# A four-layer graph network on one core: layers 0, 2 and 3 add their edges up as running sums on VectorE instead of scattering them on TensorE

## What is computed

```python
edge_index = jnp.stack([src, dst])
h = relu(layernorm(x)); x = x + L0(h, edge_attr_32, src, dst, ...)
h = relu(layernorm(x)); x = x + L1(h, ..., src, dst, edge_type_86)
h = relu(layernorm(x)); x = x + L2(h, edge_index, edge_weight, ...)
h = relu(layernorm(x)); x = x + L3(h, src, dst, ...)
# L0: msg = relu(h[src] + edge_attr);  agg = segment_sum(msg, dst);  ((1 + eps) h + agg) @ W.T + b
# L1: attention over 86 relations, 16 bases; the self loop takes the source of a node's LAST edge
# L2: msg = weight[:, None] * h[src];  agg = segment_sum(msg, dst);  relu(agg @ W + b)
# L3: msg = h[src];                    agg = segment_sum(msg, dst);  agg @ W.T + b
```

## Time and profile before

| | |
|---|---|
| median of the runs | 10135.78 us |
| the profiled execution, its own time / its span | 10080.74 us / 10078.9 us |
| busy share: PE / DVE / ACT / POOL | 43% / 44% / 22% / 66% |
| layer 0, first to last gather | 56 to 2404 us |
| layer 1 | 2404 to 5381 us |
| layer 2, first to last gather | 5381 to 7698 us |
| layer 3, first to last gather | 7740 to 10036 us |
| DMA share in the wide layers / in layer 1 | 0.09 to 0.16 / 0.74 |

### The profile page before, as it was taken

One profiled execution on the slowest core, in us unless ns is written; L12 is line 12 of the kernel. 1 busy time (PEld: TensorE's weight loads), 2 busy tenths in 40 slices (PEclk: granted clock), 3 DMA queues, 4 the chain that ended last, 5 costly groups with the idle time before them and its releaser, 6 DMA issues. The chain is left out here.

```text
span 10078.9 us, 104067 instructions
## 1 busy us (share of the span) xinstructions
PE 4355.2 (43%) x23835; PEld 3907.5 (39%) x23836; DVE 4409.0 (44%) x8833; ACT 2225.0 (22%) x5812; POOL 6679.0 (66%) x6577
## 2 busy tenths in 40 slices
PE   3444444445466666666663222222223232222333
PEld 2343443344366666666662222222222222222222
DVE  5444444444377777777774222222223122222222
ACT  1000000000377777777771000000000000000000
POOL 6666666664477777787775666666665666666665
PEclk6555555555655555555555555555555555555556
DMA  4111111111477777777772000000000000000001
GB/s 72 22 22 22 22 22 22 22 22 25 157 218 218 220 219 219 218 221 219 217 219 51 11 11 11 11 11 12 11 11 16 11 11 11 11 11 11 11 11 16
DMA packets 599592, 726.36 MB, mean 72 GB/s; under 512 B 339548, under 2 KB 433308, under 8 KB 596385
## 3 DMA queue, kind: packets, MB, share of 16 engines
q0 software_dynamic: 290064, 544.60, 22.0%
q1 hardware_dynamic: 309497, 181.39, 6.6%
HBM read 685.53 MB, written 40.64 MB: 72 GB/s over the span
## 5 line engine op out<-in xcount | busy, mean ns | idle before, releaser
L511 POOL DMA_INDIRECT lanes<-table,idx x4764 | 4510.3, 947 | 2539.4 <-issue 1430.4
L1277 PE MATMUL ps<-arena 128*128 128x128 f32 x9528 | 2376.9, 386 | 4187.7 <-issue 4124.4
L1277 PEld LDWEIGHTS ps<-arena 128*128 128x128 f32 x9528 | 2037.9, 277 | 4483.2 <-issue 4397.9
L511 POOL DMA_INDIRECT arena<-table,idx x1664 | 2050.8, 1232 | 675.8 <-issue 508.9
L987 DVE TENSOR_TENSOR ps<-ps,tabs 128x16 f32<-128x16 f32 x1191 | 210.5, 177 | 4057.4 <-remote 3303.4
L586 ACT COPY idx<-tabs 128x4 int32 (+1 forms) x1191 | 228.2, 193 | 6715.6 <-DMA lanes<-table,idx 6484.7
L992 DVE TENSOR_TENSOR arena<-ps,node 128x512 f32<-128x512 f32 (+1 forms) x1588 | 1056.8, 682 | 83.0 <-issue 82.2
L1269 PE MATMUL ps<-lanes 128*128 128x32 f32 x3328 | 791.6, 402 | 664.1 <-issue 463.5
L1269 PEld LDWEIGHTS ps<-lanes 128*128 128x128 f32 x3328 | 750.2, 330 | 691.5 <-issue 691.3
L1377 PE MATMUL ps<-t,arena 128*128 x3328 | 955.0, 402 | 0.0
L1377 PEld LDWEIGHTS ps<-t,arena 128*128 128x128 f32 x3328 | 860.0, 318 | 0.0
(11 more groups left out here) (201 smaller groups left out, 2807.1 us busy)
## 6 DMA issues: line engine op xcount, KB each, us to landing
arena<-step_rows SPq DMA_DIRECT2D x416, 256.0 KB
lanes<-table,idx POOLq DMA_INDIRECT x4764
arena<-table,idx POOLq DMA_INDIRECT x1664
table<-arena SPq DMA_DIRECT2D x24, 1088.0 KB, 5.2
lanes<-in_edge_attr SPq DMA_DIRECT2D x384, 64.0 KB
table<-h SPq DMA_DIRECT2D x18, 256.0 KB, 2.4
edge_rows<-arena SPq DMA_DIRECT2D x1, 2496.0 KB, 8.4
lanes<-self_loop_table,selfi POOLq DMA_INDIRECT x98
```

Of the source, the lines that this page charges most:

```text
L511: pool.indirect_dma_start(out=into, out_offset=None, in_=tableD[l], in_offset=bass.IndirectOffsetOnAxis(ap=index, axis=0)).then_inc(there, 16)
L1277: last = mm(ps[:, bass.ds(w[u], WB * D)], onehotw[:, k, u, :], wmsg[:, k, u].rearrange("p w f -> p (w f)"), start=False, stop=True, skip_g ...
```

## The change

The edges are dealt out anew in the wide layers. Partition p holds the run of consecutive edges p x 1563 to p x 1563 + 1562, so tile t is the t-th edge of all 128 partitions, and there are no extra tiles. Because edges are sorted by destination, each partition's edges come in runs of one node. Per tile DVE updates a row that holds four entries (`KEEP`): the running sum of the present node and the final sums of the three nodes before. With `same` = 1 if the edge's node is that of the edge before, the new row is `prev * same + terms`, where the terms are the edge's own message and the older entries moved along, times `1 - same`. In layer 0 an entry also carries the node's number and the source of its last edge (34 wide instead of 32).

ACT writes the messages into PSUM (`fill`), double buffered by lots, and the two factors into `scal`. SP stores every lot of rows to HBM (`put_sums`, 1563 x 128 rows of 544 or 512 bytes a layer). When the layer is through, 25 indirect gathers (`gather_fours`) fetch, for every four nodes, the row after the last edge that can belong to them; DVE picks the four sums out of the row (`pick`), PE adds what the next partition continues (`place_ends`) and moves the sums to blocks (`to_blocks`, 16 small matmuls a bank), and `linear` goes on as before. Which rows to fetch is found during layer 0: a comparison in 25 of its rounds and 25 extra gathers in the middle (`look_up`).

The core of it (the one-hots, masks, `scatter`, `clear`, the wide window tables and the extra tiles are gone):

```diff
-WB = 4
-WIDE_LOTS = -(-(TILES + EXW) // HB)
+KEEP = 4
+QB = -(-BLOCKS // 4)
+WIDE_LOTS = -(-TILES // HB)
+WIDTH = {0: D + 2, 2: D, 3: D}
 # VectorE
-            def masks(l, i, k):
-                dve.wait_ge(wide_mm_done, lots_to(l, i, k))
-                tt(mask[:, k], ..., ALU.is_equal).then_inc(masked, 1)
-            def body3(i, lots_):
-                for k in range(lots_):
-                    masks(3, i, k)
-                    onehots(i, k, onehotw)
-                    rows_there(3, i, k)
-                    dve.wait_ge(masked, lots_to(3, i, k))
-                    spread(k, grow, mask)
+            def chain(l, i, k):
+                w = WIDTH[l]
+                dve.wait_ge(filled, i * RING + (BEFORE[l] + k + 1 + RING))
+                if l:
+                    dve.wait_ge(ring_moved[k], written_count(l, i, k))
+                for u in range(tiles_of(i, k)):
+                    prev = ringA[l][:, k, u - 1] if u else ringA[l][:, (k - 1) % RING, HB - 1]
+                    terms = new(l, k)[:, u // 2, u % 2]
+                    dve.wait_ge(link, link_count(l, i, k, u))
+                    ts(terms[:, w:KEEP * w], prev[:, 0:(KEEP - 1) * w], scal[:, k, 1, u:u + 1], None, ALU.mult
+                       ).then_inc(link, 1)
+                    dve.wait_ge(link, link_count(l, i, k, u) + 1)
+                    stt(ringA[l][:, k, u], prev, scal[:, k, 0, u:u + 1], terms, ALU.mult, ALU.add).then_inc(link, 1)
 # ScalarE
+            def fill(l, i, k, ahead):
+                act.wait_ge(wide_gathered[k], gathered_count(l, i, k))
+                if ahead:
+                    wide_lot(i, k + RING)
+                act.wait_ge(link, link_count(l, i, k - 1, 0))
+                m = same[:, bass.ds(i * ROUND + k * HB, HB)]
+                nc.scalar.copy(scal[:, k, 0, :], m)
+                nc.scalar.activation(scal[:, k, 1, :], m, ACT.Relu, scale=-1.0, bias=ones[:, 0:1])
+                ...
+                    nc.scalar.copy(to[:, :, :, 0:D], grow[:, k].rearrange(...)).then_inc(filled, 1)
 # SyncE
+            def put_sums(l, i, k):
+                w, nt = KEEP * WIDTH[l], tiles_of(i, k)
+                sp.wait_ge(link, link_count(l, i, k, nt))
+                sp.dma_start(sumsD[l]...[:, bass.ds(i * ROUND + k * HB, nt), :], ringA[l][:, k, 0:nt]
+                             ).then_inc(ring_moved[k], 16)
 # GpSimd
-                        pool.wait_ge(total_ready if l == 0 else wide_msg_ready, n)
+                        pool.wait_ge(total_ready if l == 0 else filled, n)
+            def gather_fours(l):
+                for k in range(RING):
+                    pool.wait_ge(ring_moved[k], 16 * (1 + (TURN[l] + 2) * (ROUNDS + (1 if k < REST else 0))))
+                for b in range(BANKS):
+                    for B in fours_of(b):
+                        pool.indirect_dma_start(out=fours[l][:, B, :], ..., in_=sumsD[l], in_offset=...rowE[:, B:B + 1]...)
 # TensorE
-            def scatter(l, i, k, w):
-                pe.wait_ge(wide_msg_ready, i * RING + (BEFORE[l] + k + 1 + RING))
-                for u in range(HB):
-                    last = mm(ps[:, bass.ds(w[u], WB * D)], onehotw[:, k, u, :], wmsg[:, k, u]..., start=False, ...)
+            def to_blocks(l, b):
+                pe.wait_ge(quads_ready, PICKS[l] + b + 1)
+                clear(b)
+                ... for q in range(4): for i in range(4):
+                            last = mm(to, spread_of(q, i), quads[:, i, B[0]:B[-1] + 1], start=False, ...)
```

More of the change, by code:

```diff
@@ L118, in gnn @@
         tT = sb("tT", [P, GROUPS * P])
[L120 to L130, removed]
+        tabs = sb("tabs", [P, 2, STEPS_N])
+        idxS = sb("src_rows", [P, T4], I32)
+        same = sb("same", [P, T4], BF16)
+        wgt = sb("wgt", [P, T4])
+        has_edge = sb("has_edge", [P, QB * 4])
+        selfi = sb("selfi", [P, QB * 4], I32)
+        RSRC, DST, ETY = range(3)
         window = sb("window", [1, STEPS_N], I32)
@@ L537, in _ @@
                         narrow(n)
+                    continue
+                if l == 0:
+                    with pool.Fori(0, FOUND_ROUND) as i:
+                        wide(i, RING)
+                    look_up()
+                    with pool.Fori(FOUND_ROUND, ROUNDS) as i:
+                        wide(i, RING)
                 else:
@@ new lines, in wide_layer, with add @@
+            def wide_layer(l):
+                zero_sums(l)
+                with dve.Fori(0, ROUNDS) as i:
+                    for k in range(RING):
+                        chain(l, i, k)
+                for k in range(REST):
+                    chain(l, ROUNDS, k)
+            def add(i, k):
+                dve.wait_ge(wide_gathered[k % RING], gathered_count(0, i, k))
+                dve.wait_ge(ring_moved[k % RING], written_count(0, i, k))
+                dve.wait_ge(filled, i * RING + (k + 1 + LOTS))
+                tt(total[:, k % LOTS], grow[:, k % RING], attr[:, k % RING], ALU.add).then_inc(total_ready, 1)
@@ new lines, in compare, with rounds0 @@
+            def compare(i, k):
+                if k == 0:
+                    ts(compared, ends, thr4[:, bass.ds(i, 1)], None, ALU.is_lt).then_inc(compare_done, 1)
+                if k == RING // 2:
+                    dve.wait_ge(compare_done, i + 1)
+                    nc.vector.reduce_sum(tile4[:, bass.ds(i, 1)], compared, AX.X).then_inc(compare_done, 1)
+            def rounds0(i, n, also=None):
+                for k in range(n):
+                    if also:
+                        also(i, k)
+                    if not isinstance(i, int) or i * RING + k + 1 < WIDE_LOTS:
+                        add(i, k + 1)
+                    chain(0, i, k)
@@ L1297, in transposes, with sources_to_blocks @@
+            def sources_to_blocks():
+                pe.wait_ge(quads_ready, BANKS + 1)
+                clear(7)
+                for q in range(4):
+                    for i in range(4):
+                        last = mm(ps[:, SRC7:SRC7 + 4 * QB].rearrange("p (B q) -> p B q", q=4)[:, :, q], spread_of(q, i),
+                                  fours_src[:, i], start=False, stop=True, skip_group_check=True)
+                last.then_inc(permuted, 1)
             def transposes(of, b):
@@ L1303, in _, with linear @@
             tf, hf = (v[:, :, :].rearrange("p b f -> p (b f)") for v in (t, h))
-            def linear(q, w, bias):
+            def linear(q, w, bias, l=None):
+                if l is not None:
+                    place_ends(l)
+                    to_blocks(l, 0)
+                    to_blocks(l, 1)
                 for turn in range(BANKS + 1):
+                    if l is not None and turn + 2 < BANKS:
+                        to_blocks(l, turn + 2)
+                    if l == 0 and turn + 2 == BANKS - 1:
+                        sources_to_blocks()
                     if turn < BANKS:
```

795 lines of the change are left out of this document (443 added, 352 removed).

## The result

The changed kernel takes 10393.6 us (median of 4 runs, 10392.5 to 10412.6), the kernel before 10136.6 us beside it (4 runs, 10115.1 to 10140.4): ratio 1.0262, 95% interval 1.0244 to 1.0281, slower. The forecast was 10331 us. The profiled execution has a span of 10391.9 us for 10078.9, +313 us, so the 55 us between the old profile and its median have no counterpart here.

The account below looks back on a forecast made before the run. POOL's gather stream, 1.25 us apart with holes, was taken to bound the kernel. Gathers -26, ends +180, `look_up` +31 and preparation +10 gave +195 on 10081, 10276; plus 55 for the median, 10331 us, range 10110 to 10750.

Parts of the forecast that it names:

- The chain: DVE's two dependent instructions a tile, 285 and 266 ns: 2.4 to 2.8 us a lot, hidden behind POOL's 5.0.
- The slow lot: DVE's cost of four tiles while instructions issue late in the wide layers: 8.5 to 10 us, against 2.4 to 2.8 otherwise.
- The gaps of 0.5 us: Sign in DVE's instruction stream: gaps by "issue" when instructions come late, against 0.03 us in fast phases.
- The pace: Wide-layer gathers stay at 1.479 us each including holes: 4689 gathers take 6935 us, -26 us; bounds 1.25 and 1.75.
- The ends: Between a layer's last gather and the next layer's first: 100 us for 42.5, +58 a layer, +180 with layer 0's sources.
- the drain of the backlog with the last store: At a wide layer's end, DVE finishes up to 8 lots and the last store lands: 12 + 2 us.
- PE as the end's bound: At a layer's end PE's moving of sums, 8.4 us a bank, outlasts DVE's picks, 6.2: 50 us for six banks.
- Preparation: Work before layer 0's first tile, whose parts change: +10 us, between -10 and +30.
- The 55 us added for the median: Whole kernel: the median of the runs lies 55 us above the profiled execution, so 10276 became 10331 us.
- Rival A: Wide layers: with PE silent the slow phases go, 1.25 us a gather, 9186 us in all; chance 0.28.
- Rival B: Wide layers: DVE's issue falls to about 1 us an instruction, a lot takes 7 us, 11580 us in all; chance 0.13.
- Rival C: Whole kernel even: 1.446 us a gather and ends at +135 give 10111 us, the forecast's lower edge; no separate chance.

Follow-up runs that it names:

- the pauses: Changed kernel with a POOL memset of 256, 512 or 1024 columns after each lot's wide gathers: 10284.7, 10529.9 and 11035.8 us for 10071.3 of the kernel before.
- second profile: The changed kernel run again unedited, beside the kernel before on the same chip: 10341.1 us for 10084.5, ratio 1.0254.
- the second set: Runs with lighter POOL pauses in both kernels, or the changed kernel with fewer rows, instructions or stores; unpaused kernel before 8911.0 us, paused 8995.0.

## Why the prediction was right, and where it was off

The direction, the range and the main reading were right: POOL's stream stays, its stops stay, and the ends pay. The forecast of 10331 us was 63 us low, which is the sum of misses of both signs.

- Gathers, 1563 a layer at 947 ns and 1.25 us apart: right.
- The chain. 0.61 us a tile was forecast, 0.74 measured (323 and 350 ns for 266 and 285), 3.0 us a lot for 2.4 to 2.8. Hidden as said. The borrowed prices came from instructions with other operand mixes. The Trainium skill ("VectorE: DVE Perf Modes", the errata of SBUF-source operations) would make it 225 and 258 ns for 96 and 128 elements, as an estimate by the 120 cycles that its table gives from PSUM to SBUF; layer 2's rows say 321 and 347. The update reads PSUM and writes SBUF, the product goes the other way, for which the table has no row. Its warning of a fixed cost per instruction agrees with the trace, and the cost here is larger.
- The slow lot. 8.5 to 10 us was forecast from 0.5 us an entry; with 0.7 us an entry and 1.43 us a waiting instruction it is 7 x 1.43 + 4.5, about 14.5 us, and 14.1 is the median. The share of slow time, taken over as 0.8, fell to 1550/2344 = 0.66. The two misses largely cancelled, which is luck: with both put right the prediction's formula gives 1/(0.66/14.1 + 0.34/3.0) = 6.2 us a lot in layer 2, where 5.6 was forecast and 6.0 measured. The gaps of 0.5 us that it named as a sign of slow phases are 1.05 to 1.08 us.
- The pace. 1.479 us was forecast; 1.494 to 1.504, 1.500 and 1.471 came, +44 us over three layers. The reason, "the gathers more than the load", is half right. The run written out on DVE shows that load counts: fewer entries per lot gave 1.437 and 1.417. That the old and the new kernel have one pace is chance to that extent. What the gathers do set is whether slow phases come at all, as the pauses show.
- The ends, the term of the sum that was mis-sized: +180 forecast, 68 + 93 + 81 = +242 measured. After layer 2, 100 us became 136. The step that failed is the drain of the backlog with the last store, 35 us for 14: DVE was some nine lots behind, the first part of it still slow, the rest at 3.0 us a lot. Where there are no slow phases that term is 9 us and the end 102 to 109, near the 100 forecast. The gathers of fours themselves came as priced (32.5 us for 31) though the first took 3.13 us; a pick took 7.0 us for 6.2, its sums 0.95 us each for 0.69. PE as the end's bound: shown, by cutting it.
- `look_up`: +31 forecast, 31 measured (1492.0 to 1522.0 us, 25 gathers, and the step on). Preparation: +10 forecast, +2 measured. Layer 1: +18 not forecast; the same kernel's second profile has 2623 us where the first had 2649, so it is scatter.
- The 55 us added for the median: not there, 54 us too many. With the ends (+62), the pace (+44), layer 1 (+18) and the preparation (-8) this gives the 63.

Rival A fell: PE made no record in the loops of layers 2 and 3 and the slow phases stayed; in the second set PE had all its work and there were none. Its price did show, 1.25 to 1.28 us a gather, but in both kernels. Rival B fell as a pace (5.96 us a lot, not 7), though its price of a slow lot, 17 us, was nearer to 14.1 than mine. Rival C fell with the ends. Three slips in the working change nothing above: the earlier trace rows give 120 to 190 PE records a round, loads included, and not 120 to 240, and A's 9186 us and B's 11580 count the -26 us of the gathers twice.

What stays open: what it is behind POOL's gathers that holds up the other queues, why it does so on some occasions only, and whether it goes by gathers or by rows. Instruction fetch is made unlikely by the written-out run, which has some four thousand rows of straight code on DVE in a layer and is faster.

## What to carry to other kernels

When all engines but one show short instructions far apart with "issue" before them, look at the register operations of their queues. If these too take much longer than their median, suspect the engine that still runs at full pace, and test it by slowing that engine. Here that cost layer 2 nothing where slow phases occur (2317 us for 2344), and 84 us of a launch where they don't. Moving work off a busy-looking engine gains nothing while another's stream sets the pace; price what the new scheme adds between stages, and start with the backlog that must drain there. Compare with the old kernel of the same occasion only: it moved by 13% between occasions.

## What the runs showed of the hardware

- With indirect gathers of 128 rows of 128 bytes issued every 1.25 us, nearly each entry of the DVE, ACT and SP queues came to cost about 0.7 us, 22 us after a layer's first gather and mostly 9 to 11 us after later restarts; PE's loads and products in a slow phase of the kernel before came about 1.4 us apart, though the register operations recorded on its queue took some 0.04 us. At 1.42 us a gather there was no slow phase over 2216 us. In one of the four sets there was none at 1.25 us either.
- Layer 1's preparation meets it as well: its 98 gathers of each node's own row at 1.25 us run beside PE's products. Windows of the changed kernel's second profile, while they run and after:

```profile
2559.00:2680.00 121.00, 17.47 (x91) 9.90 (x89) 9.52 (x39) 11.41 (x22) 91.66 (x97) 0.53 0.16 41
2680.00:2774.00 94.00, 63.60 (x526) 46.54 (x526) 55.62 (x273) 56.73 (x127) 0.95 (x1) 0.87 0.65 263
```

  PE made 91 matmul records in the first 121 us and 526 in the next 94; the granted clock was 0.53 in the first, near its 1.2 GHz level, and 0.87 in the second, between that and the 2.4 GHz level. In the set without slow phases the second stretch is gone: PE made 644 records in the 125 us of the gathers, and layer 1's first gather came 2 us after the last of the 98, for 94.
- A DVE sum over 512 strided elements to 128 took 0.95 us; four products of 512 elements took 2.50 us together.
